# First attention of a four-stage kernel: keys projected once for two neighbouring groups, and their other half brought over by DMA

## The reference, cut to what matters

```python
q = (x @ Mq).reshape(B, H, C, K)      # B 4, C 1024, H 8, K 64, width 128
k = (x @ Mk).reshape(B, H, C, K)
v = (x @ Mv).reshape(B, H, C, V)      # V 16
scores = jnp.einsum('bhqk,bhck->bhqc', q, k).reshape(B * H, C, C)
att = jax.nn.softmax(scores / jnp.sqrt(jnp.float32(K)), axis=1)
att4 = att.reshape(B, C, H, C)
out = jnp.einsum('bqhc,bhcd->bqhd', att4, v)
```

## Time and profile before

| What | us |
|---|---|
| median of three runs | 1932.06 |
| lowest and highest | 1929.78, 1940.83 |
| the profiled execution, its own time | 1930.25 |
| its span, first to last instruction | 1928.5 |
| first attention stage, from its first instructions to the last sum on DVE | 24 to 522 of the span |

### The profile page before, as it was taken

One profiled execution on the slowest core, in us unless ns is written; L12 is line 12 of the kernel. 1 busy time (PEld: TensorE's weight loads), 2 busy tenths in 40 slices (PEclk: granted clock), 3 DMA queues, 4 the chain that ended last, 5 costly groups with the idle time before them and its releaser, 6 DMA issues. The chain is left out here.

```text
span 1928.5 us, 39668 instructions
## 1 busy us (share of the span) xinstructions
PE 1630.0 (85%) x14336; PEld 901.3 (47%) x14337; DVE 1319.5 (68%) x1787; ACT 1274.3 (66%) x2303; POOL 476.2 (25%) x656
## 2 busy tenths in 40 slices
PE   5999999999979999999999999699997436704870
PEld 4555655555543443344444444377772112304860
DVE  2667677676679999999999994245554596341445
ACT  2777777777738898998989997378885760402221
POOL 0222222222162000000000000189991232042006
PEclk8999999999969999999999998599998768857995
DMA  5000000000013100110010000164300000412013
GB/s 203 2 0 0 0 0 0 0 0 0 1 36 99 28 16 2 23 24 1 16 28 5 2 1 1 44 148 97 93 17 14 1 0 0 151 34 77 23 30 84
DMA packets 42890, 62.64 MB, mean 32 GB/s; under 512 B 7768, under 2 KB 28000, under 8 KB 42016
## 3 DMA queue, kind: packets, MB, share of 16 engines
q1 hardware_dynamic: 38688, 55.97, 10.5%
q0 software_dynamic: 4096, 5.25, 1.0%
HBM read 34.85 MB, written 9.57 MB: 23 GB/s over the span
## 5 line engine op out<-in xcount | busy, mean ns | idle before, releaser
L862 ACT ACTIVATE m_probs<-m_ring 128x512 f32<-128x512 f32 x1024 | 545.8, 595 | 97.9 <-PE m_ring L776 81.5
L928 DVE TENSOR_REDUCE m_half_max<-m_pairs 128x2 f32<-128x1024 f32 x512 | 587.8, 1217 | 13.9 <-PE m_pairs L759 12.8
L351 DVE TENSOR_REDUCE a_neg_max<-a_scores 128x1 f32<-128x1024 f32 x257 | 310.5, 1215 | 118.6 <-PE a_scores L287 118.5
L341 ACT ACTIVATE a_probs<-a_scores,a_neg_max 128x1024 f32<-128x1024 f32 x256 | 285.3, 1114 | 127.2 <-DVE a_neg_max L351 127.2
L776 PE MATMUL m_ring<-m_q_max,m_k 32*128 32x512 f32 x1024 | 330.8, 505 | 5.8 <-DVE m_q_max L942 4.0
L791 PE MATMUL m_acc<-m_probs,m_v_aug 128*32 128x256 f32 (+1 forms) x4032 | 332.1, 403 | 0.0
L759 PE MATMUL m_pairs<-m_k,m_q 32*128 32x512 f32 x1024 | 263.3, 511 | 13.3 <-DVE m_half_max L928 9.6
L776 PEld LDWEIGHTS m_ring<-m_q_max,m_k 32*128 32x128 f32 x1024 | 152.4, 185 | 226.7 <-ACT m_probs L862 131.1
L287 PE MATMUL a_scores<-a_q,a_k 64*128 64x512 f32 x1032 | 257.2, 617 | 0.9 <-ACT a_probs L341 0.9
L386 POOL TENSOR_TENSOR a_scaled<-values,a_inv 128x128 f32<-128x128 f32 x256 | 102.7, 401 | 417.6 <-DVE a_inv L369 283.9
L1323 POOL TENSOR_TENSOR e_g_parts<-e_gated,e_g_parts 128x512 fp32r<-128x512 f32 x128 | 164.7, 1321 | 16.5 <-ACT e_g_parts L1269 15.6
(11 more groups left out here) (254 smaller groups left out, 1848.3 us busy)
## 6 DMA issues: line engine op xcount, KB each, us to landing
e_gates<-sorted_results SPq DMA_DIRECT2D x64, 256.0 KB, 3.7
m_k<-m_k_init SPq DMA_DIRECT2D x8, 512.0 KB, 8.8
m_q<-xT SPq DMA_DIRECT2D x8, 512.0 KB, 10.3
sorted_tokens<-xT SPq DMA_DIRECT2D x5, 512.0 KB, 6.0
f_sorted_rows<-sorted_tokens SPq DMA_DIRECT2D x10, 256.0 KB, 4.9
sorted_results<-f_out SPq DMA_DIRECT2D x10, 256.0 KB, 2.2
e_w<-e_w_dram SPq DMA_DIRECT2D x1, 2064.0 KB, 7.8
xT<-x_t_dram SPq DMA_DIRECT2D x1, 2048.0 KB, 7.6
```

The costliest lines, as they stand in the source:

```text
L341: nc.scalar.activation(probs[:, g, :], scores[:, slot(h * G + g), :], ACT.Exp, bias=neg_max[:, g:g + 1], accum_out=total[:, g:g + 1]).then ...
L351: nc.vector.tensor_reduce(neg_max[:, i % G:i % G + 1], scores[:, slot(i), :], AX, ALU.max, negate=True).then_inc(max_done, 1)
L862: nc.scalar.activation(probs[:, u % SLOTS, head, :], ring[:, bank, :], ACT.Exp, scale=0.5).then_inc(ring_taken, 1)
L928: nc.vector.tensor_reduce(half_max[:, pair // PAIRS % 2, at:at + 2], pairs[:, pair % 2, :, :], AX, ALU.max).then_inc(pair_taken, 1)
```

## The change

The keys of two neighbouring groups, 2j and 2j+1, are now made by one product, so that the even group's keys come out in partitions 0 to 63 and the odd group's in 64 to 127. Four products, one projection and one copy (`k_own`) make the keys of a tile. SP then issues two DMAs per tile, each of 64 partitions by 2 KB (128 KB), which bring `k_own`'s halves to the opposite halves of `k_other`. A score product takes `k_own` where the group's keys stand in its own half, and `k_other` where not.

The keys are now projected first (round 0), the queries second (round 2), and rounds 4 and 6 hold no projection. ACT copies the keys behind exp of g = 2 and the queries behind exp of g = 4. The first score of a tile waits for the queries' copy and for the tile's two DMAs. The loads for the next stage are issued one per tile, behind the tile's two DMAs, over the first 13 tiles. `w_k` is half as large.

```diff
+    DUP = 32
-        k = core.sb("a_k", [D, 2, G, TILE], F32, st)
+        k_own = core.sb("a_k_own", [D, 2, G // 2, TILE], F32, st)
+        k_other = core.sb("a_k_other", [D, 2, G // 2, TILE], F32, st)
...
             @block.sync
             def _(sp):
-                for to, at in loads:
-                    sp.dma_start(to, at).then_inc(loaded, 16)
+
+                def double(head, p):
+
+                    sp.wait_ge(keys_copied, head + 1)
+                    for h in range(2):
+                        sp.dma_start(k_other[64 - 64 * h:128 - 64 * h, p, :, :],
+                                     k_own[64 * h:64 * h + 64, p, :, :]).then_inc(keys_doubled, 16)
+
+                double(0, 0)
+                for head in range(TILES):
+                    double(head + 1, (head + 1) % 2)
+                    if head < len(loads):
+                        to, at = loads[head]
+                        sp.dma_start(to, at).then_inc(loaded, 16)
+                sp.wait_ge(keys_doubled, DUP * (TILES + 1))
                 sp.wait_ge(loaded, 16 * len(loads))
...
+                def project_keys(head):
+                    pe.wait_ge(queries_copied, head)
...
+                def project_queries(head):
+                    pe.wait_ge(keys_copied, head + 1)
...
                     if g == 0:
-                        pe.wait_ge(copied, COPIES * head + 2)
-                    if g == 4:
-                        pe.wait_ge(copied, COPIES * head + 3)
+                        pe.wait_ge(queries_copied, head + 1)
+                        pe.wait_ge(keys_doubled, DUP * head + DUP)
                     pe.wait_ge(exp_done, CREDIT + n - back(i) + 1)
                     for h in range(2):
                         rows = slice(64 * h, 64 * h + 64)
-                        last = nc.tensor.matmul(scores[:, slot(i), h * BANK:(h + 1) * BANK], k[rows, p, g, :],
+                        keys = k_own if g % 2 == h else k_other
+                        last = nc.tensor.matmul(scores[:, slot(i), h * BANK:(h + 1) * BANK], keys[rows, p, g // 2, :],
                                                 q[rows, p, :, :].rearrange("p g t -> p (g t)"), start=True, stop=True)
...
-                for c in range(COPIES):
-                    project(0, c)
+                project_keys(0)
+                project_queries(0)
...
-                            if g < 2 * COPIES:
-                                project(head + 1, g // 2)
+                            if g == 0:
+                                project_keys(head + 1)
+                            if g == 2:
+                                project_queries(head + 1)
...
-                            if g in (3, 5, 7):
-                                copy(head + 1, (g - 3) // 2, (h + 1) % 2)
+                            if g == 2:
+                                copy_keys(head + 1, (h + 1) % 2)
+                            if g == 4:
+                                copy_queries(head + 1, (h + 1) % 2)
...
-                w_k = core.sb("w_k", [D, G, TILE], F32, st2)
+                w_k = core.sb("w_k", [D, G // 2, TILE], F32, st2)
...
-    def doubled(w):
-        w = w.reshape(D, G, 64)
-        return np.ascontiguousarray(np.concatenate([w, w], axis=2))
+    def neighbours(w):
+        return np.ascontiguousarray(w.reshape(D, G // 2, TILE))
```

More of the change, by code:

```diff
@@ L221, in first_attention_stage @@
     HB, HEADS_OF = 3, 4
-    COPIES = 3
+    DUP = 32
     with ExitStack() as st:
@@ L236, in first_attention_stage @@
         zeroed = core.sem("a_zeroed")
-        projected = core.sem("a_projected")
-        copied = core.sem("a_copied")
+        keys_projected = core.sem("a_keys_projected")
+        keys_copied = core.sem("a_keys_copied")
+        keys_doubled = core.sem("a_keys_doubled")
+        queries_projected = core.sem("a_queries_projected")
+        queries_copied = core.sem("a_queries_copied")
         scores_done = core.sem("a_scores_done")
@@ L268, in _, with tokens @@
             def _(pe):
-                def project(head, c):
-                    pe.wait_ge(copied, COPIES * head + c)
-                    at = ds(PAD + head * TILE, TILE) if not isinstance(head, int) else slice(PAD + head * TILE, PAD + (head + 1) * TILE)
+                def tokens(head):
+                    return ds(PAD + head * TILE, TILE) if not isinstance(head, int) else slice(PAD + head * TILE, PAD + (head + 1) * TILE)
+                def project_keys(head):
+                    pe.wait_ge(queries_copied, head)
                     for j in range(4):
-                        w = w_q[:, j, :] if c == 0 else w_k[:, 4 * (c - 1) + j, :]
-                        last = nc.tensor.matmul(proj[:, j * TILE:(j + 1) * TILE], w, xT[:, at], start=True, stop=True)
-                    last.then_inc(projected, 1)
+                        last = nc.tensor.matmul(proj[:, j * TILE:(j + 1) * TILE], w_k[:, j, :], xT[:, tokens(head)],
+                                                start=True, stop=True)
+                    last.then_inc(keys_projected, 1)
+                def project_queries(head):
+                    pe.wait_ge(keys_copied, head + 1)
+                    for j in range(4):
+                        last = nc.tensor.matmul(proj[:, j * TILE:(j + 1) * TILE], w_q[:, j, :], xT[:, tokens(head)],
+                                                start=True, stop=True)
+                    last.then_inc(queries_projected, 1)
                 def score(i, head, n):
@@ L325, in _, with copy_keys, copy_queries @@
             def _(act):
[L326 to L329, removed]
+                def copy_keys(head, p):
+                    act.wait_ge(keys_projected, head + 1)
+                    nc.scalar.activation(k_own[:, p, :, :].rearrange("p g t -> p (g t)"), proj[:, :],
+                                         ACT.Copy).then_inc(keys_copied, 1)
+                def copy_queries(head, p):
+                    act.wait_ge(queries_projected, head + 1)
+                    nc.scalar.activation(q[:, p, :, :].rearrange("p g t -> p (g t)"), proj[:, :],
+                                         ACT.Copy).then_inc(queries_copied, 1)
                 act.sem_inc(exp_done, CREDIT)
-                for c in range(COPIES):
-                    copy(0, c, 0)
+                copy_keys(0, 0)
+                copy_queries(0, 0)
                 with act.Fori(0, TILES - HEADS_OF + 1, HEADS_OF) as first:
@@ L2347, in layouts @@
         "w_q": halves(f["L0_attn_Mq"]),
-        "w_k": doubled(f["L0_attn_Mk"]),
+        "w_k": neighbours(f["L0_attn_Mk"]),
         "w_v": np.ascontiguousarray(f["L0_attn_Mv"]),
```

## The result

The changed kernel takes 1911.1 us (median of 4 runs, 1908.9 to 1911.8) beside 1935.0 for the kernel before, timed with it (4 runs, 1929.8 to 1940.8): a ratio of 0.987, 95% interval 0.984 to 0.991. It is faster, by some 24 us or 1.3%, and 9 us above the forecast of 1902, a little outside the range. The profiled execution took 1908.85 (span 1907.1).

The account below looks back on a forecast made before the run. PE, gapless in the stage, was taken as the bound: 34.9 - 8.8 + 1.9 + 0.7 = 28.7 us off 1930.25 gives 1901.6, said as 1902. This case reaches 1898 to 1906; the stated range is 1892 to 1910.

Parts of the forecast that it names:

- The projection that goes: PE in the stage's loop: 32 projections of 1.09 us leave its stream, saving 34.9 us if PE stays gapless.
- the buffers at the end of a body: Last tile of each of eight loop bodies: PE waits 1.10 us for exp to release score buffers, 8.8 us given back.
- The other tiles: Tiles not last in a body: buffers are released just in time for the shorter rounds, so no cost.
- the 0.09: Spare in us in ordinary tiles: PE can go on at 4.76 and wants to at 4.85.
- The moved copies: ACT's keys' and queries' copies push exp 3 to some 4.15 and exp 5 to 8.18; nothing late, nothing gained.
- The two DMAs: Each tile's pair lands 2.2 us after its second issue, with 6.4 us available: no cost.
- The start of the stage: Before the loop: two projections instead of three precede the first score, at 35.5 instead of 37.46; 1.9 us gained.
- The first load: Loads at kernel start: 256 KB less of `w_k` at 350 GB/s saves 0.7 us, possibly 0.
- the sum: Whole kernel: 34.9 - 8.8 + 1.9 + 0.7 = 28.7 us off the profiled 1930.25, giving 1901.6.
- The rivals: Alternatives: no loss at body ends 0.08; spare fails 0.12, more lost 0.03; late DMAs 0.06; score products not parallel 0.03.
- The second: Rival: rounds 4 and 6 run at 3.1 to 3.3 us, 24 tiles lose 7 to 17 us, 1909 to 1919; chance 0.12.

Follow-up runs that it names:

- e3: Changed kernel with e2's wait, score buffers' order shifted to a round with a projection, keys' copy one exp later; median 1901.9 us, stage 456.29.
- e4: Changed kernel with e2's wait, plus four unused products in round 4 of each loop body's last tile; median 1908.5 us, stage 464.8.
- e6: Changed kernel with e2's wait, without the two DMAs per tile, both halves of a score reading their own half's keys; stage 464.0 us.
- e12: Changed kernel with 96 semaphore increments on PE during the first loads; with e13, four of eight runs below all 15 of the changed kernel.
- e14: Kernel before with 160 semaphore increments on PE during the first loads; start deducted, no run below 1939.8 us.
- e1: Kernel before, with GpSimd's split of the expert weights made to wait for VectorE's gates; median 1930.9 us, ratio 0.998.
- e2: Changed kernel, with GpSimd's split of the expert weights made to wait for VectorE's gates; median 1901.5 us, ratio 0.982 to the kernel before.
- e11: Changed kernel, unchanged, run again beside the kernel before; none of the changed kernel's 15 runs in all is below 1908.4 us.
- e9: Kernel before, unchanged, for a second profile; 22.4 us from SP's first issue of the expert weights to PE's first gate product.
- e13: Changed kernel with 85 semaphore increments on PE during the first loads; first score 2.9 us later; with e12, four of eight runs below the changed kernel's 15.

## Why the prediction was right and wrong

- **The projection that goes** (34.9), **the buffers at the end of a body** (8.8 back): right. The loop gives 26.1 of 26.1, and in the stage e3 and e4 show the 8.8 from both sides.
- **The other tiles**: the 0.09 holds. A tile that is not the last takes 13.89 (167.24, 181.13 and 195.02 start the same projection), the last of a body 14.99 (195.02 to 210.01).
- **The moved copies**: exp 3 starts 4.02 behind its round where some 4.15 was said; nothing is late.
- **The two DMAs**: cost nothing in the loop, 2.3 us where 2.2 was taken. At the start they were to be covered and are not: the first score comes 5.60 behind the first projection, 5.37 without DMAs (e6), so by this pair of runs it waits 0.2 for the DMAs. By the Trainium skill (SBUF — State Buffer, "Door 1: The DMA port swizzle" and "Can I just issue two DMAs to hit both halves?"), as the prediction's estimate, the pair would land 3.3 behind the first issue. Measured is 2.9 behind the copy, which is nearer to the 2.8 that the row gives with an issue of 0.57.
- **The start of the stage**: mis-sized, 1.1 for 1.9. The first score comes 1.77 sooner behind the first projection, but the scores then take 6.21 until the loop's first projection, where they had taken 5.56. The clock does not come sooner with them. Before and after it rises a little past 39 us (windows of 38 to 40, columns as in the earlier trace rows, before and then after), so more of the scores run at 0.50 now. The prediction had left that out:

```profile
38.00:39.00 1.00, 1.00 (x4) 0.34 (x2) 0.00 (x0) 0.16 (x1) 0.00 (x0) 0.50 0.97 397
39.00:40.00 1.00, 1.00 (x6) 0.38 (x4) 0.56 (x1) 0.00 (x0) 0.00 (x0) 0.94 1.07 426
```

```profile
38.00:39.00 1.00, 1.00 (x4) 0.29 (x2) 0.94 (x2) 0.50 (x3) 0.00 (x0) 0.50 0.00 0
39.00:40.00 1.00, 1.00 (x6) 0.21 (x2) 0.72 (x1) 1.00 (x2) 0.39 (x1) 0.98 0.06 16
```

- **The first load**: 0.5 of 0.7. The terms of the sum thus give 27.7 of 28.7, and only the 1.35 of the values' products, a chance of the two profiles, bring the stage to 29.1: that nearness is luck. Over more profiles it holds to about a microsecond. The layer norm behind the stage begins at 521.1 to 522.1 in three profiles with the old loop and at 492.7 to 494.2 in five with the new one, on average 28.2 apart.
- **The step that failed is the sum.** "1930.25 ... : 1901.6": it takes over the whole rest of the program as it stood in one execution, and the case's own range, 1898 to 1906, holds nothing for it. In the rest a race between VectorE and GpSimd, won in that execution at 0.00 us, is worth 6.7 to 11 us to the gate; it is lost in all three profiles of the changed kernel, since the change took some 90 instructions out of PE's stream and with them moved the code fetch that had held the loads back (e12 to e14). With the split made to wait, the time is 1901.5 where 1902 was forecast for the kernel without that wait.
- **The rivals**: none came true. The second names the right time, 1909 to 1919, by a mechanism that the trace excludes. That the median of before stood 1.8 above the profiled execution was taken as noise; over 62 runs it is 4.6, and that was the sign that something in the rest of the program comes out differently from run to run.

## What to carry to other kernels

Work out the stage, and then look through the rest of the program for races that it won by less than a microsecond: two engines that use the same memory at once, with nothing that orders them. A change far ahead of them can turn them, as it did here by moving a code fetch. Where such a pair is found, an explicit wait cost nothing here (e1 0.998) and takes the race out of the time, though not the scatter of the clock; a saving should be compared with that wait in both kernels. Where work leaves a software pipeline, look at which buffer distance it had covered: shifting the order of three buffers by four and one copy by a group (e3) gave back in the stage all that the shorter rounds had lost. The whole time shows it in two runs of five (1892.8 and 1893.0); by the median, 1901.9, e3 is no faster than e2.

## What the hardware showed unasked

- VectorE beside a GpSimd split of 128 x 2048: an addition of 128 x 32 took 4.37 us instead of 0.19, a product of 128 x 256 4.60 (e11) instead of 0.43.
- The clock of PE falls to its lower level behind the first attention, for a stretch of 37.5 us in eleven profiles, 41.0 in two, 54.6 in e2 and 58.0 in e4 and e9. In e2, e4 and e9 SP's first issue of the expert weights comes 726.5 to 726.8 us behind the first product of the layer norm, in the others 717.5 to 721.9. I found nothing that sets the long ones. The windows of the kernel after, then of e2:

```profile
550.00:570.00 20.00, 20.00 (x169) 7.21 (x165) 17.92 (x18) 15.69 (x30) 8.13 (x18) 0.80 0.74 228
```

```profile
550.00:570.00 20.00, 20.00 (x122) 6.33 (x119) 15.08 (x14) 12.96 (x24) 9.56 (x20) 0.50 0.73 231
```

- This explains e2's profiled execution of 1909.4, where its other four runs took 1900.6 to 1902.2. That e3 has runs at 1892.8 to 1893.0 and at 1901.9 to 1902.0 fits it, but rests on the mean granted clock of the runs alone: 0.907 and 0.908 in the two short ones, 0.903 and 0.904 in the three long ones, which have no profile.
- Two DMAs of 128 KB between the halves of the partitions: 2.3 us from the second issue until PE can use them.
- A semaphore increment on PE took 0.15 us. From the first to the last, 160 of them took 24.4 us (e14, 0.83 to 25.19), and the first product starts at 25.57 in e14, 15.79 in e12 (96) and 14.13 in e13 (85). What lies beyond the loads' 12.67 or 12.15 is the delay.
